# One DMA instead of three for each pair of down-projection weights, in a transformer block with two mixture-of-experts layers

## The reference, cut to what matters

```
x = x + 0.5 * ffn(layernorm(x), ...)
x = x + attn(layernorm(x), ...)
x = x + 0.5 * ffn(layernorm(x), ...)
```

```
h = silu(buf @ w_gate[e]) * (buf @ w_up[e])     # buf 96x512, w_gate, w_up 512x192
out = h @ w_down[e]                             # w_down 192x512
y[tok] += weight * out                          # scattered back to the rows
```

## Time and profile before

| | us |
|---|---|
| median of three runs | 1342.84 |
| the runs | 1337.5 to 1356.78 |
| the profiled execution, its own time | 1337.5 |
| its span, first to last instruction | 1335.3 |
| FFN 1, from the first load that waits for a buffer (pair 6) to the first wave of attention matmuls | 137 to 415 |
| FFN 2, from the same load to the end of the last scatter | 1028 to 1306 |

### The profile page before, as it was taken

The page is one execution under the profiler, slowest core; times in us unless marked ns, Lnnn a source line. Parts: engine busy times, 40 slices in busy tenths (PEclk is TensorE's granted clock), DMA queues, the critical chain, the costliest instruction groups (busy, mean ns, idle before and its releaser), DMA issues.

```text
span 1335.3 us, 26235 instructions
## 1 busy us (share of the span) xinstructions
PE 1204.0 (90%) x10296; PEld 778.2 (58%) x10296; DVE 623.8 (47%) x1154; ACT 512.6 (38%) x1302; POOL 500.5 (37%) x407
## 2 busy tenths in 40 slices
PE   7999999898886889999999999999998998989870
PEld 5535776666664656655655665565336776667640
DVE  6993222221214767767777676624980222221220
ACT  3312111111111477887798788641122111111100
POOL 0033455555542363432333232000304555555544
PEclk9999999999998999999999999998998999999995
DMA  9997999999997954444344543233745999999977
GB/s 350 346 400 247 284 338 336 329 329 330 329 279 208 312 124 98 102 103 122 105 111 104 135 105 78 80 111 136 291 171 167 336 337 340 330 323 339 327 178 134
DMA packets 164633, 307.30 MB, mean 230 GB/s; under 512 B 19616, under 2 KB 52768, under 8 KB 164512
## 3 DMA queue, kind: packets, MB, share of 16 engines
q1 hardware_dynamic: 130896, 237.53, 53.8%
q0 software_dynamic: 23808, 57.69, 18.5%
q10 hardware_dynamic: 9808, 10.42, 2.3%
HBM read 222.47 MB, written 61.87 MB: 213 GB/s over the span
## 4 chain that ended last, share of the span: by engine, by line
PE 52%; DMA 26%; DVE 10%; issue 4%; ACT 4%; POOL 2%; SPq 0%; ACTq 0%; POOLq 0%; DVEq 0%
DMA ya_d<-osb,tok 9%; PE ps L369 9%; DMA out<-osb,tok 9%; PE ps L385 5%; PE ps L434 5%; PE ps L477 4%; PE ps L465 4%; PE ps L445 4%; PE ps L491 4%; DMA yc_d<-osb,tok 3%; DMA buf<-xn_d,tok 3%; PE ps L420 2%; PE ps L317 2%; PE ps L316 2%; PE ps L528 2%
## 5 line engine op out<-in xcount | busy, mean ns | idle before, releaser
L369 PE MATMUL ps<-bufT,gu 128*64 128x96 f32 x6144 | 294.6, 257 | 11.6 <-issue 7.8
L369 PEld LDWEIGHTS ps<-bufT,gu 128*64 128x64 f32 x6144 | 284.6, 174 | 20.6 <-issue 10.0
L1035 DVE TENSOR_SCALAR osb<-ps,gt 96x512 f32<-96x512 f32 x128 | 93.8, 745 | 246.8 <-PE ps L385 100.4
L1118 DVE TENSOR_REDUCE Mx<-ps 128x1 f32<-128x512 f32 x256 | 170.7, 684 | 73.3 <-PE ps L445 73.0
L744 ACT ACTIVATE ps<-ps,Mx 128x512 f32<-128x512 f32 x256 | 174.8, 685 | 37.5 <-DVE Mx L1118 36.8
L699 ACT COPY bufT<-ps 128x384 f32<-128x384 f32 x128 | 60.9, 478 | 325.4 <-PE ps L352 325.4
L385 PE MATMUL ps<-wd,h 64*96 64x512 f32 x768 | 180.4, 602 | 4.0 <-DVE osb L1035 3.7
L757 ACT ACTIVATE PT<-ps 128x512 f32<-128x512 f32 x256 | 158.4, 619 | 47.8 <-PE ps L465 45.3
L1247 POOL DMA_INDIRECT buf<-xn_d,tok x128 | 127.7, 998 | 94.6 <-issue 57.7
L1028 DVE TENSOR_TENSOR h<-sg,ps 128x288 f32<-128x288 f32 x64 | 29.1, 454 | 221.8 <-PE ps L369 221.7
L445 PE MATMUL ps<-St 96*128 96x512 f32 x256 | 118.3, 479 | 9.0 <-ACT ps L744 6.7
(11 more groups left out here) (157 smaller groups left out, 1571.5 us busy)
## 6 DMA issues: line engine op xcount, KB each, us to landing
gu<-in_L_ffn_w_gate SPq DMA_DIRECT2D x64, 768.0 KB, 16.2
gu<-in_L_ffn_w_up SPq DMA_DIRECT2D x64, 768.0 KB, 20.4
wd<-in_L_ffn_w_down SPq DMA_DIRECT2D x192, 256.0 KB
St<-HL SPq DMA_DIRECT2D x186, 128.0 KB, 2.3
wqk<-wp_d SPq DMA_DIRECT2D x32, 512.0 KB, 5.2
xn_d<-XN SPq DMA_DIRECT2D x24, 256.0 KB, 4.5
X<-in_L_attn_X SPq DMA_DIRECT2D x4, 1024.0 KB, 10.5
ya_d<-X SPq DMA_DIRECT2D x4, 1024.0 KB, 18.4
```

What stands on the lines that cost most here:

```text
L369: t = e.matmul(bk[64 * k:64 * k + 64, CAP * j:CAP * j + CAP], gu[:, 2 * k + m, c, j:F:3], f.bufT[(2 * q + k) % 4][:, c, :], start=(c == 0) ...
L1035: e.tensor_scalar(f.osb[x % 4][:, :], bank(4 + x % 2)[0:CAP, :], f.gt[:, x % 8:x % 8 + 1], None, ALU.mult).then_inc(f_ev, 1)
L1118: e.tensor_reduce(Mx[:, qt, hl:hl + 1], bank((4, 5, 7)[n % 3]), AX, ALU.max, negate=True).then_inc(a_max, 1)
```

## The change

The three DMAs for `wd` become one that covers all three rows, and the wait in `pe_down` counts one DMA for a load where it counted three.

```diff
@@ pe_down @@
-            e.wait_ge(s_dn[q % NR], loaded(f, 2 * q, 3))
+            e.wait_ge(s_dn[q % NR], loaded(f, 2 * q, 1))
@@ load @@
-            for j in range(3):
-                e.dma_start(wd[:, j, :], w_down[x].rearrange("x (p j) h -> (x p) j h", j=3)[:, j, :]).then_inc(s_dn[q % NR], 16)
+            e.dma_start(wd[:, :, :], w_down[x].rearrange("x (p j) h -> (x p) j h", j=3)).then_inc(s_dn[q % NR], 16)
```

## The result

The changed kernel takes 1359.03 us against 1340.17 us before (medians; four runs each). The ratio is 1.0136, with a 95% interval from 1.0094 to 1.0179. The forecast was 1344 us with a range of 1326 to 1372 and "within 2%". The time went in the forecast direction, but 19 us up where I had worked out about 1 us. The term for the scatters was too small, and what PE loses at the gathers and in the first pairs was not in the sum.

The account below looks back on a forecast made before the run. DMA engines shared by loads and scatters were taken as the bound; cheaper loads and slower scatters gave 2.2 us earlier in FFN 1, 3.3 later in FFN 2, together +1.1 us: 1344 us on the median, range 1326 to 1372.

Parts of the forecast that it names:

- The term for the scatters: Scatters beside the loads: larger load packets hold the other queue up longer; 0.3 us lost per scatter.
- the sum: Both expert stages from pair 8: FFN 1 2.2 us earlier, FFN 2 3.3 us later, together +1.1 us.
- The loads' work: Weight loads on q1: fewer fixed packet costs save 0.22 us a pair, bringing the work to 6.53 us.
- Rows stay whole: wd loads on q1: a 6144 B row goes as one packet; mean near 3400 B, near 7300 packets per 100 us.
- the rival in which nothing happens: Loads beside scatters: bytes set the rate, or rows are cut again; 1343 us, chance 0.12.
- one-to-one turns: DMA engines alternate packet by packet between queues: 37 ns for each of a scatter's 7 packets per engine, 0.26 us.
- "up to 0.2": A gather's 5 packets per engine ahead of a scatter add up to 0.2 us to that scatter.
- SP and the end of the loads: SP issue savings count 0; loads take 9.3 to 9.5 us a pair and end some 12 us earlier in both stages.
- my signs of being wrong: Scatters of 8.1 or less or 9 and more, loads waiting for buffers late, q1 mean under 3000 B, or L385 awaiting weights.
- "Gain only": Expert stages: packets cost less and scatters stay at 8.1 us; ends 7.2 and 1.1 us earlier, 1335 us, chance 0.22.
- "scatters slowed in proportion": Scatter chain on POOL's queue: up to 1.7 us more a scatter; 1359 us at +0.85, 1391 at +1.7; chance 0.16.
- point of decision: Slowed-scatters rival: from about +1.2 us a scatter on, the kernel is slower by over 2%.

Follow-up runs that it names:

- 2048 B, one DMA: Changed kernel, still one DMA per wd load, but a partition's three rows written in reverse order so they cannot merge; ratio 0.9998 to the kernel before.
- 2048 B, then 6144 B: Changed kernel with one DMA per wd load, 2048 B rows for pairs 0 to 19 and 6144 B for pairs 20 to 31; ratio 0.9975 to the kernel before.
- the same, second timing: Kernel with 2048 B wd rows for pairs 0 to 19 and 6144 B after, timed again with more rounds; ratio 1.0034 to the kernel before.
- 6144 B, loads held back: Changed kernel, SP holding each load back by one more pair from pair 12 and two from pair 22; ratio 1.0108 to the kernel before.
- 6144 B, then 2048 B: Changed kernel with one DMA per wd load, 6144 B rows for pairs 0 to 19, 2048 B for pairs 20 to 31; ratio 1.0042 to the kernel before.

## Why the prediction was right in kind and short in size

Scatters of the chain in us (their number), and the two stages together from the first down matmuls to the last, in one trace each:

| `wd` rows (gate and up 3072 B but where said) | 137 to 200 us | 1100 to 1240 us | both stages |
|---|---|---|---|
| 2048 B, before | 8.06 (7) | 8.40 (16) | 537.0 |
| 2048 B, one DMA | 7.97 (7) | 8.27 (12) | 536.0 |
| 2048 B, then 6144 B | 8.01 (7) | 8.37 (8) | 537.2 |
| the same, second timing | 8.01 (7) | 8.33 (16) | 541.8 |
| 4096 and 2048 B | 8.04 (2) | 8.11 (16) | 535.2 |
| 2048 B, gate and up 1536 B | 7.78 (7) | 8.20 (5) | 540.2 |
| 1024 B | none | 7.77 (6) | 547.8 |
| 6144 B, the change | 8.50 (5) | 8.42 (8) | 550.6 |
| 6144 B, loads held back | 8.46 (7) | 8.64 (13) | 547.7 |
| 6144 B, then 2048 B | 8.53 (5) | 8.26 (16) | 548.4 |
| 6144 B, gate and up 1536 B | 8.67 (6) | 8.42 (6) | 549.7 |

Early in FFN 1 the 6144 B rows part the kernels without overlap: long rows are shown to slow the scatters there. In FFN 2 they don't, though that stage loses as much as the other. For FFN 2 the runs show that the row length costs time, and not by which step.

- *The loads' work.* Predicted 6.53 us a pair, measured 6.55. Over five kernels with whole partitions, from 1553 B at 74.8 ns to 3415 B at 152.3 ns, the line is 0.0416 ns per byte with 10.2 ns fixed; I had 0.0362 ns per byte with 14.3 ns, and 9.1 ns from a second pair, from windows without scatters. Right.
- *Rows stay whole.* The mean of 3415 B and 7218 packets (forecast near 3400 and 7300) rule out the rival in which nothing happens.
- *The scatters' time.* I took 0.3 us, near the one-to-one turns. Measured: 0.44 early, and 0.6 from 200 to 300 us (8.78, seven, against 8.18). This is the term that was mis-sized. Its ground also failed: the run with a short mean and long `wd` rows has the slow scatters, so it isn't the mean packet that counts.
- *The gathers.* The sum had no term for them but "up to 0.2" ahead of a scatter, from 5 packets per engine. A gather has 4: from 110 to 125 us before, q0 moves 1.54 MB, seven gathers of 96 rows of 2304 B, in 440 packets. In the chain of FFN 1 the gathers go from some 7.5 to 8.1 us, and PE waits 41.1 us for them instead of 32.0. With scatters, gathers and the longer L369 groups PE's pace in FFN 1 goes from 8.87 to 9.49 us (pairs 8 to 22), where I had 9.17. In FFN 2 it goes from 9.19 to 9.51 (pairs 8 to 27). The 9.49 forecast there was met by luck: it was 0.3 us of slower scatter, and the scatters show 0.02. Of the 6.1 us that these 19 pairs lose, 2.5 stand between the transposes and 3.3 in L369 groups and up to the down matmuls.
- *The first eight pairs.* The sum started at pair 8 as if nothing could happen before. But these pairs took 66.7 and 66.5 us instead of 63.9 and 64.0. In FFN 1, 0.9 us of it is a wait for a gather, which now comes too late for PE, and 1.9 us is longer L369 groups; in FFN 2 all of it is in L369 groups, with the stops above. No group of down matmuls comes late after its gate and up group. In the two traces with long rows and no stops (loads held back, long rows early) these pairs take 65.3 to 66.8 us, by waits for gathers of 1.4 to 2.9 us. With long rows and whole partitions it is 65.3 to 69.2 in all other runs as well; in five of the seven profiled executions with rows up to 4096 B early on, it is 63.9 to 64.1, in the other two, of one set of runs, 65.1 to 66.4. This missing term is up to 5.3 of the 13.6 us, and how much of it is the row length's and how much the stops' is not shown.
- *SP and the end of the loads.* I wrote that the loads stay late and end 12 us earlier. They aren't late at all, and the last one goes out 9.6 and 5.4 us sooner after pair 0. Loads that wait for buffers late in a stage were one of my signs of being wrong, and it came true in both stages. The gain is where I put it, at the end of each stage, 2.9 and 1.2 us.
- *The rivals.* "Gain only" is out. In "scatters slowed in proportion" I had +16 us for +0.85 us a scatter; the measured +19 us came with half of that, since gathers and the first pairs were missing there too. Its point of decision, +1.2 us a scatter for 2%, probably lay too high. That the time lies in the range is owed to the upper end, which was set by this rival and not by the sum.

## What to carry to other kernels

Where bulk loads and a chain of small dependent transfers share the DMA engines, the row length of the loads is a trade: long rows are cheaper for the loads, and they hold up the others. Here rows of 2048 to 4096 B are the flat bottom, 1024 B rows of `wd` or 1536 B rows of gate and up give the scatters time back and seem to take it from the loads, and 6144 B rows cost 1.4%. Read such a change from both sides, and count every queue whose transfers someone waits for, gathers too.

## What had not been expected of the hardware

- Splitting a load by partitions, 64+64 or 48+48+32 rows, cost 7.3% to 8.1% of the kernel, far more than anything done to row length.
- SP's hold-up doesn't go with the bytes: with 976 packets per load SP's lag grew to 21 us, with 944 in one DMA for `wd` to 18 us, with 832 (4096 and 2048 B rows) to 12, with 688 it stayed at 0.1. The number of packets alone doesn't give it either: 1232 packets (6144 and 1536 B rows) came to 13 us.
- Early in FFN 1 a scatter lost 0.44 us while the packets of its queue stayed at 150 to 154 ns. What it waits for between them is not shown, nor why rows of 6144 B do it and rows of 4096 B don't.
- PE stopped for 0.1 to 0.4 us in the middle of a group of matmuls, for nothing that the profile shows, 19 times in the changed kernel and never in the kernel before or in eight of the others. The rows don't decide it.
